# A decoder block with a routed expert layer: router moved into the cross-attention stage, token rows gathered in place of scattered

## The chip, the cores and the metric

The kernel runs on one core of a Trainium2 chip. The metric is the device time of one execution in microseconds (us), as the median of repeated runs. Within 0.2% a run of this kernel can't be told from no change.

## The reference

32 sequences of 112 tokens, 512 channels, all f32:

```python
x = x + attn(layernorm(x))                    # windowed attention, 16 heads of 32
x = x + xattn(layernorm(x), ctx_1024)         # 16 query heads of 128, 8 key heads, 375 context rows of 256
h = layernorm(x).reshape(-1, 512)             # 3584 tokens
probs = softmax(h @ wg)                       # wg: 512 x 8
idx = argmax(probs);  gate = probs[idx]
x = x + gate * (h @ W[idx].T + b[idx])        # W: 8 x 512 x 512, one expert per token
```

## The kernel before

The program is three functions, one after the other, each a block of its own: on every engine its instructions are written out in order, and between functions all engines meet at a barrier and the semaphores are cleared.

`window_attention` does the first line in 8 turns of 4 sequences and stores the sum `x1` and its normalized transpose `h2T` in DRAM. Beside that it clears things for the last stage: `clear_slots` stores 1032 KB of blank rows into `slots` once in each turn.

`cross_attention` (L847) goes twice over the 32 sequences, 8 query heads in each half, so 64 batches of 4 steps, 256 steps. A product is made of three passes over high and low halves of its operands. A step has on TensorE, in this order: the scores of 2 heads (`scores`), the K projection of the next batch (`early_fills`), a part of the output projection of a finished 128-token tile (`rows`, with the parts placed by `ROWS_AT`), the product with V of step i - 2 (`pv`), further fills (`late_fills`, `before_transposes`), the transposes of the probabilities of step i - 1 (`probsT`), and at times one more fill behind them (`behind_transposes`). Fills are the transposes of the context (C, only in the first half), and the projections K, V and Q. They go in turns through two PSUM banks, in the fixed list `ORDER`: a fill waits on TensorE until the one two places before it has been copied out by ScalarE (high half) and VectorE (low half). The two context transposes of a batch are one in step g = 2 and one in step g = 3. `HEAD` is what is made before step 0. `splits_at` spreads the splitting of weights into halves; the output weights are split in batch 0. The softmax goes from VectorE (`maxima`) to GpSimd (bias), ScalarE (`exps`), VectorE (`inverses`), GpSimd (L1201, two multiplications) and back to TensorE. When a tile's output projection is whole, `add` (L1307) adds it to `sums`; in the first half the sum is kept in `x1_half`, in the second half it goes to `x2`. All its loads and stores are issued by SyncE, in a loop over batches: `load_base`, `load_x`, `load_ctxT`, `store`, `load_mask`, and others, each behind its wait.

`expert_ffn` (L1533) has two blocks. The first reads `x2` back (28 tiles of 128 tokens, loops over pairs), normalizes it (L1736 to L1757), transposes it (L1862) and multiplies it with `wg` (L1872, f32, 8 columns); it finds the expert, the gate and the slot of each token in a chain of small VectorE operations (L1809 to L1846) in which each waits for the one before; scatters the 28 tiles of token rows with GpSimd to `slots` in DRAM, sorted by expert (L1683); and beside that loads, transposes and splits the expert weights `W` in 32 units of 256 KB through 4 buffers (L1624, L1888, L1702, L1779). The second block loads the 35 slots of 128 rows with SyncE (L1966), normalizes (L2008), transposes (L2052), splits (L1996, L2013), multiplies with the expert's weights (L2063), adds bias (L2023), gate and residual (L2028), and scatters the result to `out` (L1980).

```python
                        sp.dma_start(rows[:, k, :], slots_t[bass.ds(n, 1)].rearrange("a p c -> (a p) c")) \
                            .then_inc(rows_in[k], 16)
                        if is_first(turn, k, U) and k == 3:
                            sp.dma_start(bias[:] ...
```

## Time and profile before

| | us |
|---|---|
| median of 3 runs (2679.69 to 2681.14) | 2681.05 |
| the profiled execution, its own time | 2699.72 |
| its span, first to last instruction | 2698.0 |
| TensorE matmul busy | 2495.8 (93%) |
| TensorE weight loads busy | 2270.3 (84%) |
| VectorE busy | 1743.5 (65%) |
| ScalarE busy | 1248.4 (46%) |
| GpSimd busy | 1014.3 (38%) |
| mean DMA rate | 81 GB/s |

PE is TensorE's matmuls, PEld its weight loads, DVE VectorE, ACT ScalarE, POOL GpSimd, SP SyncE, and SPq SyncE's queue of DMA issues. PEclk is the granted TensorE clock, 1.00 being 2.4 GHz and 0.50 being 1.2 GHz. In a timeline row the numbers are the start and the length in us, then engine, line, operation, what it writes<-what it reads, the count, and in brackets the engine's idle time just before and what ended it.

### The profile page before, as it was taken

Reading aid. Unit: us, or ns where it says so; the run is one execution under the profiler, and the core shown is the slowest. Engines: PE = TensorE matmul, PEld = TensorE weight load, DVE = VectorE, ACT = ScalarE, POOL = GpSimd, SP = SyncE. Lnnn points to the kernel's source line nnn. Section 1 sums busy time; section 2 is a strip of 40 time slices with the busy share of each in tenths; the row PEclk is TensorE's granted clock in tenths of the full one; section 3 lists DMA queues with packets and bytes.
Section 4 is the critical chain, followed back from the end, with each engine's and each line's share of the span. In section 5 each row is a group of like instructions: output and inputs, shape, how many; then the busy total and the mean of one; then the engine's idle time right before and its main releaser. Section 6 shows DMA issues by size and latency. Waiting matters only on the chain. (4 is left out here: it accounts for less than half of the span.)

```text
span 2698.0 us, 46191 instructions
## 1 busy us (share of the span) xinstructions
PE 2495.8 (93%) x14850; PEld 2270.3 (84%) x14851; DVE 1743.5 (65%) x4871; ACT 1248.4 (46%) x3155; POOL 1014.3 (38%) x1424
## 2 busy tenths in 40 slices
PE   6999997699999999999999999999999999979388
PEld 5888886589998998999888889989999998969276
DVE  6878886475666657565666657566575656654466
ACT  4545554354544545454554545454454545522211
POOL 3434443043333434343333434344343434431422
PEclk9999999899999999999999999999999999985699
DMA  7322232422121221121132212111121111122654
GB/s 255 95 70 84 93 103 93 142 62 66 56 62 48 87 66 59 55 73 66 49 107 61 82 50 61 50 53 58 41 66 54 41 58 50 44 70 75 217 178 129
DMA packets 110493, 217.89 MB, mean 81 GB/s; under 512 B 20400, under 2 KB 50832, under 8 KB 110016
## 3 DMA queue, kind: packets, MB, share of 16 engines
q1 hardware_dynamic: 105040, 188.42, 22.3%
q0 software_dynamic: 5040, 16.58, 1.6%
q10 hardware_dynamic: 224, 10.49, 1.2%
q8 instruction: 105, 1.72, 0.3%
q14 instruction: 84, 0.69, 0.1%
HBM read 134.57 MB, written 91.36 MB: 84 GB/s over the span
## 5 line engine op out<-in xcount | busy, mean ns | idle before, releaser
L1201 POOL TENSOR_SCALAR x_probs<-x_probs,x_inv 112x376 f32<-112x376 f32 x512 | 634.6, 1249 | 196.0 <-DVE x_inv L1352 196.0
L1245 ACT ACTIVATE x_probs<-x_probs,x_bias 112x376 f32<-112x376 f32 x512 | 307.9, 602 | 426.8 <-POOL x_bias L1195 426.8
L1195 POOL TENSOR_SCALAR x_bias<-x_top 112x1 f32<-112x1 f32 x512 | 118.0, 230 | 973.8 <-DVE x_top L1324 973.8
L1410 PE MATMUL x_ps_f<-x_xT,x_wq 128*128 128x448 f32 x1536 | 342.4, 373 | 7.1 <-DVE x_wq L1292 6.4
L1456 PE MATMUL x_ps_r<-x_wo,x_oT 128*128 128x512 f32 x1344 | 345.6, 393 | 2.3 <-DVE x_wo L1292 1.4
L1410 PE MATMUL x_ps_f<-x_wv,x_ctxT 128*128 128x512 f32 (+1 forms) x1152 | 308.5, 405 | 25.4 <-DVE x_kT L1302 22.8
L1410 PEld LDWEIGHTS x_ps_o<-x_pT,x_v 128*128 128x128 f32 (+1 forms) x2304 | 295.3, 191 | 35.2 <-DVE x_pT L1331 17.4
L1410 PE MATMUL x_ps_s<-x_kT,x_qT 128*112 128x376 f32 x1536 | 313.8, 340 | 3.0 <-DVE x_top L1324 3.0
L1410 PEld LDWEIGHTS x_ps_f<-x_xT,x_wq 128*128 128x128 f32 x1536 | 282.6, 190 | 36.1 <-DVE x_v L1302 6.9
L1410 PE MATMUL x_ps_f<-x_ctxT,x_wk 128*128 128x376 f32 x1536 | 308.7, 337 | 4.2 <-DVE x_kT L1302 3.0
L1410 PE MATMUL x_ps_o<-x_pT,x_v 128*128 128x224 f32 (+1 forms) x2304 | 300.3, 275 | 11.6 <-DVE x_pT L1331 11.6
L1456 PEld LDWEIGHTS x_ps_r<-x_wo,x_oT 128*128 128x128 f32 x1344 | 251.2, 189 | 40.7 <-DVE x_wo L1292 1.7
L1410 PEld LDWEIGHTS x_ps_f<-x_ctxT,x_wk 128*128 128x128 f32 x1536 | 271.1, 190 | 6.5 <-DVE x_kT L1302 4.8
L1410 PEld LDWEIGHTS x_ps_s<-x_kT,x_qT 128*112 128x112 f32 x1536 | 259.2, 176 | 17.5 <-issue 4.0
L1324 DVE CUSTOM_DVE_ANT_0 x_probs<-x_ps_s,x_mrow 112x376 f32<-112x376 f32 x512 | 259.0, 543 | 5.7 <-DVE x_mrow L1312 5.7
L1410 PEld LDWEIGHTS x_ps_f<-x_wv,x_ctxT 128*128 128x128 f32 (+1 forms) x1152 | 202.3, 188 | 69.3 <-DVE x_kT L1302 28.8
L1331 DVE TENSOR_TENSOR x_pT<-x_ps_t,x_pT 128x336 fp32r<-128x336 f32 x512 | 234.1, 499 | 0.1
L1302 DVE TENSOR_TENSOR x_qT<-x_ps_f,x_qT 128x448 fp32r<-128x448 f32 x128 | 80.0, 625 | 234.0 <-ACT x_qT L1221 234.0
L1349 DVE TENSOR_SCALAR x_total<-x_total 112x1 f32<-112x1 f32 x512 | 78.9, 154 | 221.6 <-ACT x_probs L1245 221.6
L1302 DVE TENSOR_TENSOR x_v<-x_ps_f,x_v 128x512 fp32r<-128x512 f32 (+1 forms) x192 | 132.8, 691 | 121.2 <-ACT x_v L1221 121.0
L1228 ACT ACTIVATE x_pT<-x_ps_t 128x336 fp32r<-128x336 f32 x512 | 202.6, 453 | 0.0
L1221 ACT ACTIVATE x_v<-x_ps_f 128x512 fp32r<-128x512 f32 (+1 forms) x192 | 115.0, 599 | 161.9 <-PE x_ps_f L1410 161.7
(186 smaller groups left out, 3833.6 us busy)
## 6 DMA issues: line engine op xcount, KB each, us to landing
x_ctxs<-x_ctxT SPq DMA_DIRECT2D x32, 752.0 KB, 4.1
x_ctxT<-x_ctxs SPq DMA_DIRECT2D x32, 752.0 KB, 4.7
x_xT<-h2T SPq DMA_DIRECT2D x16, 896.0 KB, 4.9
m_rows<-slots SPq DMA_DIRECT2D x35, 258.0 KB
slots<-w_blank SPq DMA_DIRECT2D x8, 1032.0 KB, 5.2
x_ctxn<-in_ctx_dram SPq DMA_DIRECT2D x32, 256.0 KB
m_hn<-in_L_ffn_W_dram SPq DMA_DIRECT2D x32, 256.0 KB
w_xa<-in_x_dram SPq DMA_DIRECT2D x32, 224.0 KB, 3.5
```

The source lines that it names most:

```text
L1195: pool.tensor_scalar(bias[:, m:m + 1], top[:, m:m + 1], -0.1 * NEG, -SCALE, ALU.max, ALU.mult) \
L1201: pool.tensor_scalar(probs[0:T, m, 0:SE], probs[0:T, m, 0:SE], inv[:, m:m + 1], None, ALU.mult).then_inc(normed, 1)
L1221: act.activation(dst[HI], src, ACT.Copy).then_inc(fill_hi, 1)
L1228: act.activation(pT[:, HI, :, h * T:(h + 1) * T], ps_t[h][:, 0:NKC * T].rearrange("p (c t) -> p c t", c=NKC), ACT.Copy).then_inc(pT_hi, 1)
L1245: act.activation(probs[0:T, m, 0:SE], probs[0:T, m, 0:SE], ACT.Exp, bias=bias[:, m:m + 1], scale=SCALE, accum_out=total[:, m:m + 1]).then_ ...
L1302: dve.tensor_tensor(dst[LO], src, dst[HI].bitcast(F32), ALU.subtract).then_inc(fill_done, 1)
L1324: dve.tensor_tensor_reduce(out=probs[0:T, m, 0:SE], in0=ps_s[h][0:T, 0:SE], in1=mrow[:, i // G % 2, :], scale=1.0, scalar=-3.0e38, op0=ALU ...
L1331: dve.tensor_tensor(pT[:, LO, :, h * T:(h + 1) * T], ps_t[h][:, 0:NKC * T].rearrange("p (c t) -> p c t", c=NKC), pT[:, HI, :, h * T:(h + 1 ...
L1349: dve.tensor_scalar(total[:, m:m + 1], total[:, m:m + 1], 1e-30, None, ALU.max) \
L1410: last = pe.matmul(out, w, r, start=m == 0, stop=m == len(jobs) - 1)
L1456: last = pe.matmul(ps_r[:], oT[:, a, h, slot:slot + P], wo[:, b_, h, :], start=h == 0 and (a, b_) == PASSES[0], stop=h == H - 1 and (a, b_ ...
```

## The change

- In the second half of `cross_attention` each finished tile is, in the step after `add`'s and later ones, also measured (`stats`), normalized (`rstd` on GpSimd, `normal`), transposed (fill R, one step later), multiplied with `wg` (fill L, three steps later), and its gate made (`keep_logits`, `gate_weights`, `gate`, four steps later). Row, mean, 1/deviation and gate are stored together in `x2r` (515 columns), two batches later in SyncE's loop; `load_base` comes at the end of the loop's body. R and L are fills in `ORDER` and take turns in the two PSUM banks. The last tiles are finished in a `TAIL` of seven more steps, and the logits stay in SBUF.
- Both context transposes of a batch are in step g = 2. `HEAD` makes all eight Q fills ahead of the context transposes of batch 1, and the first of them starts by chunks, each chunk of `xT` and `wq` split together. The output weights are split in batch 1.
- `expert_ffn` is one block without loops. It starts with the chain of small operations, inverts the permutation with 28 TensorE products of one-hot bf16 matrices, and gathers each slot's rows from `x2r` with GpSimd, 8 slots ahead, by the same index by which it scatters the result. `W` is loaded from the start of the block; the bias is loaded behind `W`.
- `window_attention` no longer clears `slots`; it stores four blank blocks of `x2r` and `out` near its end.

The core of the diff:

```diff
-                        if s == 2:
-                            clear_slots(turn)
...
+                for n in range(rest.shape[0] // P):
+                    sp.dma_start(blanks[n * P:(n + 1) * P, :], blank[:]).then_inc(blank_out, 16)
+                    sp.dma_start(rest[n * P:(n + 1) * P, :], blank[:, 0:C]).then_inc(blank_out, 16)
...
+    def tiles_at(i):
+
+        if i == STEPS + 2:
+            return [TILES - 1]
+        return [tile - TILES for tile, h0, h1 in (row_parts(i) if 0 <= i < STEPS else []) if h1 == H and tile >= TILES]
...
-        if g >= 2 and b + 2 < B:
-            out.append(("C", b + 2, g - 2))
+        if g == 2 and b + 2 < B:
+            out += [("C", b + 2, 0), ("C", b + 2, 1)]
         if g == 3 and b + 1 < NB:
             out.append(("V", b + 1, 0))
         if g == 1:
             out += [("V", b, c) for c in range(1, NKC)]
+        out += [("R", t, 0) for t in tiles_at(i - 1)] + [("L", t, 0) for t in tiles_at(i - 3)]
...
-        return fs if fs and fs[-1][0] == "C" else fs[:-1]
+        return fs if fs and fs[-1][0] in "CRL" else fs[:-1]
...
-    HEAD = [("C", 0, 0), ("C", 0, 1)] + [("K", 0, g) for g in range(G)] + [("Q", 0, h) for h in range(4)] + \
-           [("C", 1, 0), ("C", 1, 1)] + [("Q", 0, h) for h in range(4, H)] + [("V", 0, 0)]
-    ORDER = HEAD + [f for i in range(STEPS) for f in early_fills(i) + late_fills(i)]
+    HEAD = [("C", 0, 0), ("C", 0, 1)] + [("K", 0, g) for g in range(G)] + [("Q", 0, h) for h in range(H)] + \
+           [("C", 1, 0), ("C", 1, 1), ("V", 0, 0)]
+    TAIL = range(STEPS, STEPS + 7)
+    ORDER = HEAD + [f for i in range(STEPS) for f in early_fills(i) + late_fills(i)] + \
+            [f for i in TAIL for f in after(i)]
...
-        if b == 0:
+        if b == 1:
...
+                        t = tile - TILES
+                        sp.wait_ge(gate_ready, t + 1)
+                        sp.dma_start(result[t * P:(t + 1) * P, :], sums[:, tile % 2, :]).then_inc(stored[tile % 2], 16)
...
+                    if b - 2 in TILE_OF and TILE_OF[b - 2] >= TILES:
+                        store(TILE_OF[b - 2])
...
+                    if b in TILE_OF and TILE_OF[b] >= TILES:
+                        load_base(TILE_OF[b])
...
+                    pool.tensor_scalar(var, var, EPS, None, ALU.add).then_inc(ve_ready, 1)
+                    pool.wait_ge(ve_ready, t + 1)
+                    pool.tensor_tensor(var, var, power[:], ALU.pow).then_inc(rs_ready, 1)
...
+                    act.activation(weight_of[:], logits[:, t, :], ACT.Exp, bias=less[:, 1:2], scale=1.0,
+                                   accum_out=sums[:, t % 2, GATE:GATE + 1]).then_inc(weights_ready, 1)
...
+                        act.activation(hT, ps_f[bank_of(f)][:].rearrange("p (c t) -> p c t", c=KC), ACT.Copy) \
+                            .then_inc(hT_ready, 1)
...
+                def stats(t):
+                    row = sums[:, t % 2, :]
+                    dve.wait_ge(rows_added, TILES + t + 1)
+                    dve.bn_stats(st[:], row[:, 0:C]).then_inc(st_ready, 1)
+                    dve.wait_ge(st_ready, t + 1)
+                    dve.bn_aggr(row[:, MEAN:RSTD + 1], st[:]).then_inc(mv_ready, 1)
+
+                def normal(t):
+                    row = sums[:, t % 2, :]
+                    dve.wait_ge(rs_ready, t + 1)
+                    if t:
+                        dve.wait_ge(fill_ready, until(("L", t - 1, 0)))
+                    dve.tensor_scalar(hn, row[:, 0:C], row[:, MEAN:MEAN + 1], row[:, RSTD:RSTD + 1],
+                                      ALU.subtract, ALU.mult).then_inc(hn_ready, 1)
+
+                def keep_logits(t):
+                    dve.wait_ge(fill_ready, until(("L", t, 0)))
+                    if t:
+                        dve.wait_ge(weights_ready, t)
+                    dve.tensor_copy(logits[:, t, :], ps_f[bank_of(("L", t, 0))][:, 0:E]).then_inc(logit_kept, 1)
+                    dve.wait_ge(logit_kept, t + 1)
+                    dve.tensor_reduce(less[:, 0:1], logits[:, t, :], AX.X, ALU.max).then_inc(top_ready, 1)
+                    dve.wait_ge(top_ready, t + 1)
+                    dve.tensor_scalar(less[:, 1:2], less[:, 0:1], -1.0, None, ALU.mult).then_inc(less_ready, 1)
+
+                def gate(t):
+                    g = sums[:, t % 2, GATE:GATE + 1]
+                    dve.wait_ge(weights_ready, t + 1)
+                    dve.reciprocal(g, g).then_inc(gate_ready, 1)
...
+                    for t in tiles_at(i - 1):
+                        normal(t)
                     inverses(i)
...
+                        held = ORDER[PLACE[f] - BANKS]
+                        if held[0] == "R":
+                            pe.wait_ge(hT_ready, held[1] + 1)
+                        elif held[0] == "L":
+                            pe.wait_ge(logit_kept, held[1] + 1)
+                        else:
+                            pe.wait_ge(fill_done, halved(held))
...
+                    elif kind == "R":
+                        pe.wait_ge(hn_ready, at + 1)
+                        for c in range(KC):
+                            last = pe.transpose(out[:, c * P:(c + 1) * P], hn[:, c * P:(c + 1) * P], ident[:])
+                    elif kind == "L":
+                        pe.wait_ge(wg_in, 16)
+                        pe.wait_ge(hT_ready, at + 1)
+                        last = product(out[:, 0:E], [(hT[:, c, :], wgs[:, c, :]) for c in range(KC)])
...
+                        for c in range(KC):
+                            if n == 0:
+                                weights("q", at * QUAD // B, c)
+                                pe.wait_ge(x_lo, KC * at + c + 1)
...
+                for i in TAIL:
+                    for f in after(i):
+                        fill(f)
+                    if i == STEPS:
+                        pv(STEPS - 1)
+                        rows(HALVES * TILES - 1, 0, H)
...
+                for u in range(UNITS):
+                    e, o = divmod(u, KC)
+                    if u >= 4:
+                        sp.wait_ge(w_ready, u - 3)
+                    sp.dma_start(wn[:, u % 4, :], W[e, o * P:(o + 1) * P, :]).then_inc(w_in[u % 4], 16)
+                sp.dma_start(bias[:].rearrange("p e o -> p (e o)"),
+                             b.rearrange("e o -> (e o)").rearrange("(a n) -> a n", a=1)
+                             .to_broadcast([P, E * C])).then_inc(bias_in, 16)
...
+                def gather(k):
+                    pool.indirect_dma_start(out=rows[:, k % U, :], out_offset=None, in_=x2r,
+                                            in_offset=bass.IndirectOffsetOnAxis(ap=index[:, k:k + 1], axis=0)) \
+                        .then_inc(rows_in[k % U], 16)
...
+                for k in range(SLOTS):
+                    pool.wait_ge(y_ready, k + 1)
+                    pool.indirect_dma_start(out=out, out_offset=bass.IndirectOffsetOnAxis(ap=index[:, k:k + 1], axis=0),
+                                            in_=y[:, k % Y, :], in_offset=None).then_inc(out_done[k % Y], 16)
+                    if k + U < SLOTS:
+                        gather(k + U)
...
+                in_tile, of_tile = slotf[:, 0], slotf[:, 1]
+                link(dve.tensor_scalar(of_tile, best[:], 1.0 / P, 0.5 / P - 0.5, ALU.mult, ALU.add))
+                link(dve.tensor_scalar(of_tile, of_tile, 12582912.0, None, ALU.add))
+                link(dve.tensor_scalar(of_tile, of_tile, -12582912.0, None, ALU.add))
+                link(dve.scalar_tensor_tensor(out=in_tile, in0=of_tile, scalar=-float(P), in1=best[:],
+                                              op0=ALU.mult, op1=ALU.add))
+                dve.wait_ge(iota_done, 6)
...
+                link(dve.tensor_tensor(at_tile[:, :, 1, :], kinds[:].unsqueeze(1).to_broadcast([P, TILES, SLOTS]),
+                                       of_tile.unsqueeze(2).to_broadcast([P, TILES, SLOTS]), ALU.is_equal))
+                dve.tensor_tensor(at_tile[:, :, 0, :], at_tile[:, :, 1, :],
+                                  tile1[:].unsqueeze(2).to_broadcast([P, TILES, SLOTS]), ALU.mult)
+                link(dve.tensor_scalar(at_tile[:, :, 1, :], at_tile[:, :, 1, :], own[:, 0:1], None, ALU.mult))
+                for t in range(TILES):
+                    dve.tensor_scalar(at_lane[:, t, :], lane[:], in_tile[:, t:t + 1], None, ALU.is_equal) \
+                        .then_inc(lanes_ready, 1)
...
+                dve.wait_ge(inverted, 1)
+                a, b_ = ps_i[:, 0:SLOTS], ps_i[:, SLOTS:2 * SLOTS]
+                dve.scalar_tensor_tensor(out=found[:, 0, :], in0=a, scalar=0.0, in1=spare[:, 0:SLOTS],
+                                         op0=ALU.is_equal, op1=ALU.mult)
+                dve.tensor_scalar(found[:, 1, :], a, float(P), -float(P), ALU.mult, ALU.add)
...
+                dve.tensor_copy(index[:], found[:, 0, :]).then_inc(index_ready, 1)
+                for u in range(UNITS):
+                    low_w(u)
...
+                for u in range(4):
+                    transpose_w(u)
...
+                for t in range(TILES):
+                    pe.wait_ge(lanes_ready, t + 1)
+                    last = pe.matmul(ps_i[:, 0:2 * SLOTS], at_lane[:, t, :], at_tile[:, t].rearrange("p a k -> p (a k)"),
+                                     start=t == 0, stop=t == TILES - 1)
+                last.then_inc(inverted, 1)
+                for u in range(4, UNITS):
+                    transpose_w(u)
...
+                    pe.wait_ge(h_ready, k + 1)
+                    pe.wait_ge(w_lo, UNITS)
...
```

## Rows read from the trace of the kernel before

**Rows 1.** Busy time by stretch: PE, PEld, DVE, ACT, POOL, PEclk, DMA share, GB/s.
```profile
1370.00:2404.00 1034.00, 1014.04 (x6048) 927.81 (x6048) 652.75 (x2038) 511.26 (x1402) 419.93 (x570) 0.99 0.18 54
...
2430.00:2494.00 64.00, 62.77 (x301) 62.67 (x300) 31.50 (x96) 13.81 (x26) 10.97 (x20) 0.50 0.23 73
2508.00:2550.00 42.00, 12.46 (x53) 9.23 (x54) 9.72 (x15) 7.44 (x13) 25.97 (x27) 0.54 0.75 245
2580.00:2690.00 110.00, 108.61 (x534) 88.48 (x532) 83.63 (x134) 19.16 (x32) 32.71 (x34) 1.00 0.47 145
```

**Rows 2.** Timeline, marks of the expert stage: its start, first chain step, places, first split.
```profile
2413.05 0.20 POOL L41 MEMSET m_ident<- 128x128 f32 x1 [20.62 <-POOLq L58]
...
2495.37 0.39 DVE L1809 TENSOR_REDUCE m_best<-m_logits 128x28 f32<-128x224 f32 x1 [0.59 <-POOL m_hT L1677]
...
2505.29 0.18 DVE L1841 CAST m_slot<-m_slotf 128x28 uint32<-128x28 f32 x1
...
2507.13 2.48 DVE L1779 TENSOR_TENSOR m_wT<-m_a,m_wT 128x512 f32 x4 [0.39 <-DVE m_owner L1846]
```

**Rows 3.** Groups by line and shape: busy us, mean ns of one, idle before.
```profile
L1843 DVE TENSOR_TENSOR m_hT<-m_hT,m_number 128x280 f32<-128x280 f32 x1 | 0.4, 442 | 0.0
L1802 DVE COPY m_order<-m_before 128x128 f32<-128x128 f32 x1 | 0.2, 227 | 0.0
```

**Rows 4.** Expert weights and scatter: timeline, and one line's ns min/median/max.
```profile
2549.51 0.60 ACT L1702 ACTIVATE m_wT<-m_a 128x512 f32 x1 [1.68 <-PE m_a L1888]
...
2564.98 0.60 ACT L1702 ACTIVATE m_wT<-m_a 128x512 f32 x1 [0.54 <-PE m_a L1888]
...
L1683 POOL DMA_INDIRECT slots<-m_tokens,m_slot x28: 959/963/1227, 2506.5 to 2540.9; - x28
```

**Rows 5.** The slots: timeline of bias and first products, and the scatter's line.
```profile
2568.53 0.43 SPq L1969 DMA_DIRECT2D m_bias<-in_L_ffn_b_dram  x1
...
2577.80 0.55 DVE L2008 TENSOR_SCALAR m_h<-m_rows 128x512 f32<-128x512 f32 x1 [5.25 <-DMA m_bias<-in_L_ffn_b_dram]
...
2579.18 3.06 PE L2063 MATMUL m_y<-m_wT,m_rT 128*128 x12
...
L1980 POOL DMA_INDIRECT out_dram<-m_y,m_rows x35: 962/962/964, 2581.2 to 2691.1; - x35
```

**Rows 6.** Timeline of the head and first batch of the cross stage.
```profile
492.80 12.48 PE L1410 MATMUL x_ps_f<-x_xT,x_wq 128*128 128x448 f32 x48 [6.40 <-DVE x_wq L1292]
...
528.46 1.06 ACT L1210 ACTIVATE x_wo<-x_wo 128x1024 fp32r<-128x1024 f32 x1 [2.62 <-DMA x_wo<-own_wo]
...
533.89 2.91 PE L1410 MATMUL x_ps_f<-x_wv,x_ctxT 128*120 128x512 f32 x6 [5.19 <-DVE x_kT L1302]
```

**Rows 7.** Waits of PE, 640 to 1370, then 1370 to 2400: us, times, longest.
```profile
PE x_ps_f L1410 <- DVE x_kT L1302: 10.5, 21, 1.4
...
PE x_ps_o L1410 <- DVE x_pT L1331: 9.6, 10, 1.7
```

**Rows 8.** Timeline: router products at 1.2 GHz, then three transposes at 2.4 GHz.
```profile
2435.99 3.54 PEld L1872 LDWEIGHTS m_l<-m_wgs,m_hT 128*128 128x128 f32 x16
...
590.54 0.49 PE L1422 MATMUL x_ps_f<-x_ident,x_ctxn 128*128 128x128 f32 x3
590.87 0.74 PE L1482 MATMUL x_ps_t<-x_ident,x_probs 112*128 112x112 f32 x6
```

**Rows 9.** Timeline of one step's softmax on POOL and when TensorE takes it.
```profile
2363.87 2.48 POOL L1201 TENSOR_SCALAR x_probs<-x_probs,x_inv 112x376 f32<-112x376 f32 x2 [0.76 <-DVE x_inv L1352]
...
2369.18 0.61 PEld L1482 LDWEIGHTS x_ps_t<-x_ident,x_probs 112*128 112x128 f32 x6
```

**Rows 10.** Timeline: last output projection, and first pair of tiles from measuring to logits.
```profile
2400.71 8.36 PE L1456 MATMUL x_ps_r<-x_wo,x_oT 128*128 128x512 f32 x24 [0.87 <-DVE x_oT L1340]
...
2417.51 1.29 DVE L1736 BATCH_NORM_STATS2 m_st<-m_tokens 128x6 f32<-128x512 f32 x2 [4.33 <-DMA m_tokens<-x]
...
2429.64 0.17 DVE L1763 COPY m_logits<-m_l 128x16 f32<-128x16 f32 x1 [2.55 <-PE m_l L1872]
```

More of the change, by code:

```diff
@@ L857, in _, with cross_attention @@
                         fill(Turn(TURNS), f)
[L860 removed]
+def cross_attention(nc, B, T, S, h2T, ctx, mask, Wq, Wk, Wv, Wo, wg, base, mid, result, room):
     D = 128
@@ L1391, in _ @@
                         split(p)
+                    for t in tiles_at(i - 4):
+                        gate(t)
                 out(STEPS - 2)
                 probsT(STEPS - 1)
-                out(STEPS - 1)
-                add(HALVES * TILES - 1)
+                for i in TAIL:
+                    for f in after(i):
+                        fill(f)
+                    for t in tiles_at(i - 1):
+                        normal(t)
+                    for t in tiles_at(i - 4):
+                        gate(t)
+                    if i == STEPS:
+                        out(STEPS - 1)
+                    for t in tiles_at(i):
+                        add(TILES + t)
+                        stats(t)
             @block.tensor
@@ new lines, in expert_ffn @@
+        wn = sb("wn", [P, 4, C])
+        bias = sb("bias", [P, E, C])
+        rows = sb("rows", [P, U, R])
+        h = sb("h", [P, 2, C])
+        rT = sb("rT", [P, 2, 2, KC, P], F32R)
+        y = sb("y", [P, Y, C])
+        ident = sb("ident", [P, P])
+        owner = sb("owner", [P, SLOTS], I32)
+        index = sb("index", [P, SLOTS], U32)
+        order = sb("order", [P, TILES, E])
+        before = sb("before", [P, TILES, E])
+        like = sb("like", [P, TILES, E])
+        places = sb("places", [P, TILES, E])
@@ new lines, in expert_ffn @@
+        best = sb("best", [P, TILES])
+        chosen = sb("chosen", [P, TILES, E], BF16)
+        slotf = sb("slotf", [P, 2, TILES])
+        number = sb("number", [P, 2, 1, E])
+        start = sb("start", [P, E])
+        ownerf = sb("ownerf", [P, SLOTS])
+        steps = sb("steps", [P, SLOTS, E])
+        ends = sb("ends", [P, SLOTS, E])
+        lower = sb("lower", [P, P], BF16)
+        ones = sb("ones", [P, P], BF16)
+        lane = sb("lane", [P, P])
+        kinds = sb("kinds", [P, SLOTS])
```

813 lines of the change are left out of this document (305 added, 508 removed).

## The prediction

> **What bounds the kernel now.** I read the busy time by stretch first, then the waits inside each stretch, then timelines. The second half of the cross stage is TensorE's: matmuls are busy 1014 of 1034 us at a granted clock of 0.99, VectorE and ScalarE are at 63% and 49%, and the transfers at 54 GB/s. What is added to TensorE there costs its own time. The expert stage is another matter [rows 1]: from 2430 to 2494 TensorE is full but at 0.50, the 1.2 GHz level, with the router; from 2508 to 2550 every engine is mostly idle while DMA is busy at 0.75 (scatter and weights); from 2580 to 2690 TensorE is full again at 2.4 GHz with the slots. The marks of the stage [rows 2]: it starts at 2413.05, the chain of small operations at 2495.37, the places are written at 2505.29, and the span ends at 2698.0. So the stage lasts 285 us and 82 of them pass before its chain begins.
>
> The sum is made against the profiled execution, 2699.7 us by its own time and 2698.0 in span. The median of the runs is 2681.05, so I scale the result by 2681.05 / 2699.72 = 0.9931.
>
> **Expert stage, removed and added.** The new stage starts at once with the chain. (a) Chain to the places: 9.9 us [rows 2]; two operations go (the sum of the exponentials and its reciprocal), but they stand beside the ranking products, so I take nothing off. (b) Added behind it, all on VectorE, all waited for: four operations on 28 columns, taken at 0.2 each, 0.8; three of 128x980 at 0.442 us for 280 columns and about 1.04 ns for each further one, 1.17 each, 3.5 in sum [rows 3]; 28 comparisons of 128x128, taken like the copy of that size, 0.23 us, less what overlaps, 0.2 each, 5.6 [rows 3]; the owner's four operations, which before ended at 2507.1, 1.8; six last ones for the index, 1.1. The 28 bf16 products run beside the comparisons. So the index is ready 22.7 us after the start. Bounds: the 28 comparisons overlap fully at 0.1 us, or take 0.3 each: 20 to 26. (c) Weights: the first four units wait, transposed, for VectorE's low halves: 2.5 us. The other 28 go at the pace of the copies from 2549.51 to 2564.98, 15 units in 15.5 us or 1.03 each, 28.9 us [rows 4]. (d) The first 8 gathers are issued now. 28 scatters of the same size cost the weights a lot: from 2508 to 2550 some 8 units passed in 42 us [rows 1, 4], so (42 - 8) / 28 = 1.2 us for each DMA, which makes 9.7 for 8. At the other end it is nothing, since at the pace above the transfers had room. I take the middle, 5. Sum to the last unit: 22.7 + 2.5 + 28.9 + 5 = 59.1. (e) From the last copy of a unit (2565.6) to the second slot's product (2579.18) there were 13.6 us, of which 5.25 were VectorE's wait for the 2 MB of bias, 9.2 us after their issue [rows 5]. The bias is now issued some 4 units before the end and lands while the first product runs, so 8.3 remain. (f) From there to the end, 118.8 us, nothing changes: the slots follow each other at (2691.1 - 2581.2) / 34 = 3.23 us [rows 5], TensorE's own time at 0.99 of the stretch [rows 1]. GpSimd now issues a gather beside each scatter: 2 x (0.96 + 0.3 that I assume between two) = 2.5 us, still under 3.23.
>
> VectorE works 83.6 of the 110 us of the slots, and all 35 scatter issues lasted 962 to 964 ns [rows 1, 5]: nothing held them. Against this change speaks the Trainium skill, "SBUF — State Buffer", section "Who interferes with whom": a VectorE copy or tensor_scalar in its two-port mode locks GpSimd out, which then can't write the descriptors of its DMAs, so row loads moved from SyncE to GpSimd lose their immunity. No row shows a scatter lengthened so; what it would make is the third rival.
>
> Stage: 59.1 + 8.3 + 118.8 = 186.2 in place of 285.0: **minus 98.8**. Ends: -84 (comparisons 0.3, contention 9.7, the bias again in the way) and -107.
>
> **First half of the cross stage.** TensorE stood 6.4 us for the last piece of the first query weights and 5.2 us in batch 0, since ScalarE waited for `wo`'s transfer (2.6 us) and VectorE stood behind it [rows 6]. The first Q fill now follows the chunks (VectorE needs 1.8 us for a chunk of `xT` and `wq`), which starts it some 3 us earlier but leaves it in pieces; I take 4 for the whole head, with the value weights' split now early. The `wo` splits in batch 1 no longer wait for a transfer: 5. The V fill in step g = 3 waited for the K fill two places before it, 21 times, 10.5 us in all from 640 to 1370 [rows 7]; with C, C in g = 2 that V has free banks, and the second C comes behind the three-head part of the output projection (some 2 us of TensorE), except in batches without a tile: 8 of the 10.5. Together **minus 17**, ends 0 (the waits return one step earlier) and -25. The blank stores gone from the window stage free no engine that anyone waits for: 0; they run beside a TensorE that is busy 0.9 of that stage.
>
> **Second half of the cross stage.** Each tile adds to TensorE 4 transposes and 4 f32 products of 8 columns, which are 8 weight passes. At 1.2 GHz 16 passes took 3.54 us, 0.221 each, and at that level the weight load, not the 8 columns, is the time; at 2.4 GHz I take half, 0.11. Three transposes at 2.4 GHz took 590.87 - 590.54 = 0.33 us, also 0.11 each [rows 8]. So 12 x 0.11 = 1.32 us for a tile, and for the 26 tiles not in the tail 34.3. Low end: 9.6 us of waits for `pT` [rows 7] lie in this half and could take up 8 of it: +26. High end: the passes cost at 2.4 GHz what they cost at 1.2, 12 x 0.221 = 2.65: +69. I take **plus 35**. What hides the rest: VectorE gets 2.2 us and ScalarE 1.2 a tile in 37 us. `normal` (0.54 us, between `maxima` and `inverses`) lies where VectorE waits for ScalarE's exponentials. GpSimd's `rstd` (about 1 us) stands behind the two multiplications, and the next bias behind it, so the next softmax is 0.3 us late; the row that ends at 2366.35 is taken by TensorE at 2369.18 [rows 9], so there are 2.8 us of cover. R and L fill a bank each; a K fill behind L now waits for the K fill before it, covered by the output projection. On SyncE the store two batches later waits for a gate made in the step in which the mask load behind it waits anyway, and the base load is 2.5 steps early.
>
> **Tail.** R of tile 26 stands before the last `pv`, and the last tile has to pass through measuring, GpSimd, R, ScalarE, L, exponential, reciprocal and store before the barrier. Before, the pair of tiles took 2429.64 - 2417.51 = 12.1 us from measuring to logits [rows 10], with another pair's work between; for one tile I take 8, plus 1.2 for gate, plus L of tile 26 and its logits ahead of the last `add` 1.6, plus 2.4 for R before `pv`: **plus 13**. Base load 55 now waits for the store of tile 53, which is late, but the last projection takes 8.4 us at the low clock [rows 10] and covers it; if it doesn't, +3. Ends 9 and 17.
>
> **Sum.** -98.8 - 17 + 35 + 13 = -67.8: 2699.7 - 67.8 = 2631.9 profiled, times 0.9931 = 2613.7. I say **2613** (-2.5%).
>
> **Rivals.** First, the added weight passes or their bank waits cost double (2.65 us a tile): +34, 2647. For it: the router was only seen at 1.2 GHz. Against it: transposes do halve. Second, gathers and weights collide as the scatter did, and instruction loading with them: the weights go at a third of their pace while the gathers are under way, +15, 2628. For it: 2508 to 2550. Third, GpSimd becomes the bound of the slots: a gather takes 2 us to issue rather than 0.96, or is held up by VectorE, and the period is 3.6 in place of 3.23, from about 2.0 us per gather on; 27 slots x 0.35 = +10, 2623. Fourth, other side: TensorE stands at R for `hn`. VectorE holds `inverses` back behind `normal`, which waits for `rstd`, which waits for the multiplications; once that is longer than the 2.8 us of cover [rows 9] every tile pays. It is slower than before when a tile pays over 67.8 / 28 = 2.4 us beyond the cover; at 4 us it gives 2681 + 44 = 2725. Against it: the mean arrives in the step of `add`, and VectorE waits there anyway. Fifth, the regrouped context fills and the head bring nothing, because the wait for K moves with the C fill: 2630.
>
> **How the numbers follow.** Main case 0.58, first rival 0.12, second 0.10, third 0.05, fourth 0.04, fifth 0.11. All but the fourth are faster by over 1%. Ends of the terms: best -107 - 25 + 26 + 9 = -97, 2585; worst without a rival about -84 - 5 + 45 + 17 = -27, 2654. Not all go one way: 2590 to 2648 holds the main case, the second, third and fifth rivals and just the first. About 0.2% (5 us) is what can be told from no change. Faster 0.95, same 0.01, slower 0.04.
>
> **What would show it.** Expert stage 186 us, with the index about 23 us after its start, the last weight unit at 59, slots at 3.23, gather issues at 0.96. R and L together 1.3 us a tile at clock 1.00, and no wait of TensorE for `hn` or `hT`. Second half 35 us longer. No 5 us wait in batch 0, and few K waits from batch 2 on. The tail some 13 us longer from the last projection to the barrier. A second half longer by 60 us, a slot period over 3.3, or a weight phase of 50 us would prove steps of the sum wrong.

## The result: 48 us faster, 19 less than forecast

| | us |
|---|---|
| kernel before, median of 4 runs beside the changed one | 2680.37 (2677.56 to 2681.14) |
| changed kernel, median of 4 runs | 2632.25 (2630.38 to 2634.80) |
| ratio | 0.9817, 95% interval 0.9803 to 0.9830 |
| forecast | 2613, range 2590 to 2648 |
| changed kernel, profiled execution and its span | 2631.62 and 2629.9 |

The profile of the changed kernel, busy time by stretch (PE, PEld, DVE, ACT, POOL, PEclk, DMA share, GB/s). The stretches are the second half of the cross stage, the weights behind the index, and the slots; they answer to the first, third and fourth row of [rows 1].
```profile
1356.00:2388.00 1032.00, 1015.38 (x6186) 932.50 (x6186) 681.43 (x2160) 522.65 (x1441) 433.24 (x606) 1.00 0.17 54
2466.00:2500.00 34.00, 23.17 (x112) 16.41 (x110) 20.25 (x31) 16.73 (x28) 6.99 (x8) 0.72 0.85 286
2511.00:2621.00 110.00, 107.31 (x528) 87.46 (x526) 82.48 (x131) 19.23 (x32) 61.41 (x62) 1.00 0.46 147
```
The router's stretch at 0.50 is gone; what lies between the index and the slots is 34 us with the transfers at 0.85. GpSimd in the slots went from 33 to 61 us of 110, and TensorE stayed the bound.

Timeline marks of the expert stage, which answer to [rows 2, 5]: its first operation, the index, the last low half of a weight unit, the second slot's product.
```profile
2443.84 0.39 DVE L1834 TENSOR_REDUCE m_best<-room 128x28 f32<-128x224 f32 x1 [3.93 <-PEq L58]
...
2464.64 0.18 DVE L1893 CAST m_index<-m_found 128x35 uint32<-128x35 f32 x1
...
2499.43 0.69 DVE L1831 TENSOR_TENSOR m_wT<-m_y,m_wT 128x512 fp32r<-128x512 f32 x1 [1.06 <-ACT m_wT L1796]
...
2508.78 3.05 PE L1975 MATMUL m_y<-m_wT,m_rT 128*128 x12
```
From 2443.8, the last unit is done at 56.3 us and the second product starts at 64.9; the stage ends after 186.1.

Timeline of TensorE in one tile's part of the second half, at 2.4 GHz: the router's product (L) and what follows it, the transposes (R) and what follows them; [rows 8] had only neighbours of both.
```profile
2102.21 0.96 PE L1524 MATMUL x_ps_f<-room 128*128 128x8 f32 x8
2103.03 0.77 PE L1613 MATMUL x_ps_t<-x_ident,x_probs 112*128 112x112 f32 x6
...
2115.84 0.60 PE L1547 MATMUL x_ps_f<-x_ident,room 128*128 128x128 f32 x4
2116.28 0.74 PE L1613 MATMUL x_ps_t<-x_ident,x_probs 112*128 112x112 f32 x6
```
L takes 2103.03 - 2102.21 = 0.82 us and R 0.44, 1.26 a tile, and neither waits.

Timeline of the head and batch 0 (beside [rows 6]), and the waits of TensorE from 640 to 1360 (beside the first row of [rows 7]; us, times, longest):
```profile
492.61 18.94 PE L1573 MATMUL x_ps_f<-x_xT,x_wq 128*128 128x448 f32 x87 [0.18 <-DVE x_wq L1357]
...
524.10 1.66 PE L1524 MATMUL x_ps_f<-x_wv,x_ctxT 128*120 128x512 f32 x6 [1.77 <-DVE x_kT L1402]
```
```profile
PE x_ps_f L1542 <- DVE x_kT L1402: 6.1, 3, 2.0
PE x_ps_f L1573 <- DVE x_ctxT L1402: 5.0, 6, 0.8
PE x_ps_o L1524 <- DVE x_pT L1431: 0.7, 3, 0.3
```
The 5.2 us wait of batch 0 is 1.8 and its V fill comes 9.8 us earlier. The 21 waits of V for K are gone, but three waits of the context fill for K and six of a query fill for the context have come, 11.1 us in all where there were 10.5.

Timeline of the tail, beside [rows 10]: the last `pv`, the last output projection, the last R and the last gate.
```profile
2412.90 2.02 PE L1524 MATMUL x_ps_o<-x_pT,x_v 128*128 128x224 f32 x9 [2.65 <-DVE x_pT L1431]
...
2422.64 7.72 PE L1587 MATMUL x_ps_r<-x_wo,x_oT 128*128 128x512 f32 x24 [0.87 <-DVE x_oT L1440]
...
2434.98 1.08 PE L1547 MATMUL x_ps_f<-x_ident,room 128*128 128x128 f32 x4 [3.84 <-DVE room L1376]
...
2439.74 0.16 DVE L1392 RECIPROCAL x_sums<-x_sums 128x1 f32<-128x1 f32 x1 [0.46 <-ACT x_weight_of L1265]
```

**The two profiles set against each other.** I followed the 512 reciprocals of the softmax, one by one, through both traces. At the start of batch 2 the changed kernel leads by 10.9 us, at the start of the second half by 16.3 (1475.42 against 1491.73), at the last reciprocal it is 17.7 behind (2407.93 against 2390.28), and at the start of the expert stage 30.8 behind (2443.84 against 2413.05). The stage then takes 186.1 in place of 285.0. The spans differ by 68.1; the sum of the prediction was 67.8. Yet the medians differ by 48.1. So the sum was right against the execution that it was read from, and what needs explaining is that execution: it lasted 18.7 us longer than the median of its kernel, while that of the changed kernel lies at its median.

### The profile page after: what moved, and what is told of

It reads as the page before. It is cut to its first block and busy times, and to the rows that moved or that the text cites. A ratio compares the mean times of both kernels' runs of the same rounds, so it can differ in the third digit from the quotient of the medians.

```text
span 2629.9 us, 45420 instructions
## 1 busy us (share of the span) xinstructions
PE 2462.5 (94%) x14878; PEld 2236.7 (85%) x14878; DVE 1762.0 (67%) x4977; ACT 1259.5 (48%) x3210; POOL 1033.3 (39%) x1462
## 5 line engine op out<-in xcount | busy, mean ns | idle before, releaser
L1237 POOL TENSOR_SCALAR x_bias<-x_top 112x1 f32<-112x1 f32 x512 | 123.4, 241 | 955.6 <-DVE x_top L1424 955.3
L1573 PE MATMUL x_ps_f<-x_xT,x_wq 128*128 128x448 f32 x1536 | 343.5, 373 | 12.7 <-DVE x_ctxT L1402 5.8
L1524 PEld LDWEIGHTS x_ps_o<-x_pT,x_v 128*128 128x128 f32 (+1 forms) x2304 | 296.4, 192 | 30.4 <-DVE x_pT L1431 12.7
L1279 ACT ACTIVATE x_qT<-x_ps_f 128x448 fp32r<-128x448 f32 x128 | 69.8, 545 | 256.2 <-PE x_ps_f L1573 256.2
L1613 PE MATMUL x_ps_t<-x_ident,x_probs 112*128 112x112 f32 x1536 | 190.5, 260 | 0.0
```

What stands on the lines that cost most here:

```text
L1237: pool.tensor_scalar(bias[:, m:m + 1], top[:, m:m + 1], -0.1 * NEG, -SCALE, ALU.max, ALU.mult) \
L1524: last = pe.matmul(out, w, r, start=m == 0, stop=m == len(jobs) - 1)
L1573: last = pe.matmul(out[:, 0:T4], wq[:, a, c, n * D:(n + 1) * D], xT[:, b_, c, :], start=c == 0 and (a, b_) == PASSES[0], stop=c == KC - 1 ...
L1613: last = pe.transpose(ps_t[h][:, c * T:(c + 1) * T], probs[0:T, n % 4, c * P:(c + 1) * P], ident[0:T, 0:T])
```

## The experiments

Times are medians. Four variants shared each of three chips with runs of the kernel before: 2682.1 on the first chip (2681.0 without one of the 15 runs, which took 7992.6), 2697.3 on the second, 2679.2 on the third. Variants of the changed kernel are set against the 2632.3 us of the result, on the third chip against its 2634.0 there. Of these variants only the one of the context fills edits the part ahead of the second half; yet the profiles of the others stand 0.5 to 4.7 us behind that of the changed kernel at that point, and its own second profile 1.9. So effects of a few us are read inside the traces.

### Where the surplus of the first profile lies

**The kernel before, profiled again** (first chip), no edit.

> The kernel before, unchanged, profiled again. Its profiled execution of the prediction lasted 2699.7 us, 18.7 above the median of its runs, while that of the changed kernel (2631.6) lies at its median; against the profiled one the sum of the prediction (-67.8) meets the difference of the spans (-68.1). Theory A: the 18.7 us lie in the router's part of the expert stage, which in the first profile ran at 1.2 GHz from its start to its end (82 us before the chain); in a typical run it gets 2.4 GHz for a part of it, so that the new profile, at about 2681, has the chain some 64 us after the stage's start and everything else within 1 us. Theory B: they are spread over the cross stage and the slots (the factor 0.993 that I used); then every stretch is 0.7% shorter and the router's part is still 81 to 82 us.

The median is 2680.2, the profiled execution took 2685.4 with a span of 2683.6. Both theories fell. Every mark of the cross stage stands 1.2 to 1.3 us earlier from batch 2 to its end, a constant, so nothing is spread; and the chain starts 81.6 us after the stage's start, with the clock at 0.50 all the way. The difference is in the timeline of the weights, chain start and last low half:
```profile
2493.39 0.39 DVE L1809 TENSOR_REDUCE m_best<-m_logits 128x28 f32<-128x224 f32 x1 [0.58 <-POOL m_hT L1677]
...
2550.98 0.69 DVE L1779 TENSOR_TENSOR m_wT<-m_a,m_wT 128x512 f32 x1 [0.55 <-ACT m_wT L1702]
```
and in the busy time of 2508 to 2550, to be read beside the third row of [rows 1]:
```profile
2508.00:2550.00 42.00, 25.71 (x104) 18.79 (x102) 18.14 (x27) 15.52 (x26) 24.22 (x26) 0.52 0.94 315
```
The last unit came 58.3 us after the chain's start, against 71.1 in the first profile: 12.8 of the 14.4 us between the two spans. The same scatters were under way, but the transfers moved 315 GB/s against 245, and ScalarE made 26 copies in that stretch against 13. The waits of the same phase, the first profile's (2507 to 2566), then the second's (2505 to 2551):
```profile
PE m_a L1888 <- DMA m_hn<-in_L_ffn_W_dram: 33.6, 19, 8.7
...
ACT m_wT L1702 <- DMA x_wo<-own_wo: 16.6, 3, 9.9
```
```profile
PE m_a L1888 <- DMA m_hn<-in_L_ffn_W_dram: 15.6, 12, 3.5
```
TensorE waited 33.6 us for weights against 15.6. ScalarE's 16.6 us, put down to a transfer long done, are missing in the second; what it stood for there the trace does not say. On the second chip all nine runs of the kernel before took 2693.1 to 2698.3, so a time near that of the first profile is the rule on one chip; whether the first profile was taken on such a chip, nothing here tells. The other three runs on record with it took 2679.7 to 2681.1. The second profile too lies 5.2 us above its median, and no trace tells where.

**The kernel before without its scatters** (second and third chip).

```diff
-                    for t in range(TILES):
+                    for t in range(1):
                         pool.indirect_dma_start(out=slots, ...
-                    pool.wait_ge(scattered, 16 * TILES)
+                    pool.wait_ge(scattered, 16)
```

> The kernel before with 27 of its 28 scatters to the slots left out (the slots keep their blank rows, so the expert stage works on blanks; all its matmuls, copies and transfers are there). Both theories on the router's clock fell with the second profile of the kernel before: its router lasted 81.6 us again, all at 1.2 GHz, and the 14.4 us by which that execution was shorter lie between the chain and the last weight unit (58.3 us after the chain's start in place of 71.1), where scatters and weights run side by side. Theory A: this collision is what varies, and in a median run of before it costs some 12 us over weights alone (28 units at 1.03 us from the chain's end on, last unit some 43 to 46 us after the chain's start): the kernel without scatters takes 2664 to 2669 us. Theory B: the weights are slow there for another reason (the clock at 1.2 GHz, first instructions of the block), and nothing changes: 2680.

> The kernel before with 27 of 28 scatters left out, once more, for the case that this chip is one on which before takes 2680. Theory A as above: 2667 again whatever before takes, 13 us under a 2680 or 30 under a 2697. Theory B: it moves with before, 2650 beside a 2680.

27 of the 28 scatters are left out, so the experts work on blank rows. 2667.3 beside a before of 2697.3 (ratio 0.9890, 0.9875 to 0.9905), and 2669.4 beside 2679.2 (0.9954, 0.9939 to 0.9970). Theory A holds both times for the kernel without scatters; it had their price at some 12 us, and on the second chip it is 30. From the second chip, first and last low half, and the busy time:
```profile
2506.50 2.48 DVE L1779 TENSOR_TENSOR m_wT<-m_a,m_wT 128x512 f32 x4 [0.39 <-DVE m_owner L1846]
...
2538.89 0.69 DVE L1779 TENSOR_TENSOR m_wT<-m_a,m_wT 128x512 f32 x1 [0.65 <-ACT m_wT L1702]
```
```profile
2508.00:2550.00 42.00, 27.01 (x130) 19.43 (x128) 21.89 (x33) 17.93 (x30) 0.00 (x0) 0.80 0.71 232
```
The last unit is 44.8 us after the chain's start (2494.73). In both profiles of the kernel before, the stretch from the last unit to the end is as long as here (131.6 and 132.0 us, here 131.2), so what the scatters cost lies ahead of the last unit. So the collision of scatters and weights costs 30 us on one chip and 10 on another, and nearly all that these chips differ by in the kernel before (18 us, without scatters 2 the other way) goes with the scatters. Why it costs more on one chip, no run shows.

**The changed kernel again** (third chip), no edit.

> The changed kernel, unchanged, beside the kernel before on the same chip. The kernel before took 2680 us on the chip of the result and of its second profile, but 2697 on the chip of the last four runs, which is the time of its first profile (2700). Theory A: what differs between chips is the collision of scatters and weights alone, which the changed kernel does not have; it takes 2632 on any chip, so that the gain is 65 us beside a 2697 and 48 beside a 2680. Theory B: the chips differ in other stretches too, and the changed kernel moves with them (2648 beside 2697).

2634.0 beside 2679.2 (0.9820, 0.9806 to 0.9833); in its profile the stage takes 187.5 us, and the cross stage is 1.7 to 1.9 us later from its first softmax on. The changed kernel itself was not run on the second chip, but its variant with late gathers was, at 2633.6. That one has no gathers beside the weights; the variant with late rstd, also on the second chip, has them, and there the last unit comes 55.9 us after the stage's start, as on the first chip (56.3). So the changed kernel's time doesn't follow the chip as before's does.

### The steps of the sum

**Gathers held back** (second chip).

```diff
                 pool.wait_ge(index_ready, 1)
+                pool.wait_ge(w_lo, UNITS - 6)
                 for k in range(U):
```

> The changed kernel with its first 8 gathers held back until 26 of the 32 weight units are split. It prices the contention that the prediction put at 5 us (0 to 9.7). Theory A (the gathers cost the weights about 0.6 us each): the last weight unit comes at 51 to 52 us after the stage's start in place of 56.3, the first slot waits a little for its row, and the whole is 2 to 4 us faster, 2629. Theory B (the weights are held by their own four buffers and by SyncE): last unit still at 55 to 56, the whole 0 to 3 us slower.

2633.6. The timeline, index and last low half:
```profile
2465.82 0.18 DVE L1894 CAST m_index<-m_found 128x35 uint32<-128x35 f32 x1
...
2495.61 0.69 DVE L1832 TENSOR_TENSOR m_wT<-m_y,m_wT 128x512 fp32r<-128x512 f32 x1 [0.62 <-ACT m_wT L1797]
```
The last unit comes at 51.3 in place of 56.3 (start at 2445.0), so 8 gathers cost the weights 5.0 us, as the prediction had it (in the other profiles that keep this part as it is, the last unit comes at 55.7 to 58.3, so 4.4 to 7.0); but TensorE then waits 8.5 us for the first row, and the second product starts at 66.1, not 64.9. The size of theory A and the end of theory B.

**Context fills apart again** (first chip).

```diff
-        if g == 2 and b + 2 < B:
-            out += [("C", b + 2, 0), ("C", b + 2, 1)]
+        if g >= 2 and b + 2 < B:
+            out.append(("C", b + 2, g - 2))
```

> The changed kernel with its two context fills in the steps g = 2 and g = 3 again, as before the change. The prediction had 8 us for the regrouping. The softmaxes of the two profiles drift apart by only 2 us from batch 2 to batch 14, since waits for K in front of V (10.5 us) are gone but 11 us of waits for K in front of C and for ctxT in front of Q have come. Theory A (waits only moved): 0 to 4 us slower than the changed kernel, 2632 to 2636. Theory B (the regrouping is worth 8, and something else in the first half eats 6): 2640.

2636.8, 4.5 above the 2632.3 of the changed kernel, just above theory A's span. Its profile says more: the old wait is back to the number,
```profile
PE x_ps_f L1524 <- DVE x_kT L1402: 10.5, 21, 1.4
```
and its softmaxes fall behind those of the changed kernel from 1.7 us at the first to 8.1 in batch 34, then stay there (my expectation miscounted: its 2 us are from batch 2 to batch 28). That is 6.4, of which 3.3 come in batches 26 to 32. Two variants that leave this half alone also fell behind in it, by 2.9 us, so the regrouping is worth some 4 to 6. The span is only 4.1 us longer, since the expert stage, which the edit doesn't touch, was 2.0 shorter in this profile.

**Transposes twice, router's product twice** (first chip).

```diff
-                        for c in range(KC):
+                        for c in [c for _ in range(2) for c in range(KC)]:
                             last = pe.transpose(...
```
```diff
+                        product(out[:, 0:E], [(hT[:, c, :], wgs[:, c, :]) for c in range(KC)])
                         last = product(out[:, 0:E], [(hT[:, c, :], wgs[:, c, :]) for c in range(KC)])
```

> The changed kernel with the four transposes of each tile's normalized rows done twice. It prices the transposes in the second half. Theory A (TensorE's own time, 0.11 us a pass at 2.4 GHz): 28 x 0.44 = 12 us slower than the changed kernel, 2644. Theory B (bank waits and late softmaxes hide or double part of it): under 5 or over 20 us.

> The changed kernel with the router's product of each tile done twice (the second writes the same values). Its text has four products of 128x8, but the profile counts eight passes, 0.82 us in all. Theory A (the weight load of each pass is the time, 0.10 us, whatever the 8 columns): 28 x 0.82 = 23 us slower, 2655. Theory B (the eight columns cost little and the passes overlap their neighbours): under 12 us.

2645.0 and 2658.4, that is +12.7 and +26.1 over 2632.3, against 12 and 23. Inside the traces, over 21 tiles (batches 36 to 60), R twice costs 0.38 us a tile and L twice 0.81; 16 passes of the product in a row take 1.71:
```profile
2117.12 1.86 PE L1524 MATMUL x_ps_f<-room 128*128 128x8 f32 x16
2118.83 0.77 PE L1614 MATMUL x_ps_t<-x_ident,x_probs 112*128 112x112 f32 x6
```
Against 0.44 and 0.82 for a single set, the passes cost TensorE nearly all or all of their own time, eight columns or not. The rest of the +26.1 is 3 us that this execution was late before batch 32 already, in a part without L.

**rstd made late** (second chip).

```diff
                     pool.wait_ge(mv_ready, t + 1)
+                    for _ in range(5):
+                        idles[0] += 1
+                        pool.tensor_tensor(st[:, 6:7], power[:], power[:], ALU.pow).then_inc(idled, 1)
+                        pool.wait_ge(idled, idles[0])
                     pool.tensor_scalar(var, ...
```

> The changed kernel with five more operations of one column (powers, about 0.6 us each, 3 us in all) ahead of each tile's rstd on GpSimd. It tries the rival on the other side: normal waits for rstd on VectorE, inverses behind it, and TensorE takes the multiplied row 2.8 us after it is made. Theory A (2.8 us of cover, as in the prediction): about as slow as before by 28 x (3.0 + 0.3 - 2.8) = 14 us at most, 2632 to 2646. Theory B (the bias behind rstd has no cover, every tile pays all 3 us): 28 x 3 = 84 us, 2716.

2640.1, +7.9, theory A. In the trace the five powers (0.556 us each) cost the 24 tiles of the second half up to batch 60 only 3.0 us together, and what comes after that 3.7, most of it in the tail, where the longest wait of TensorE for a normalized tile went from 3.8 to 7.0 us:
```profile
PE x_ps_f L1554 <- DVE room L1383: 8.4, 3, 7.0
```
Another 4.6 us by which this profile is late stand ahead of the second half, where no rstd is made. The rival on the other side had cover to spare: 3 us more for each tile cost 0.13 a tile where tiles follow each other, and all 3 for the last tile, where none follows.

**GpSimd kept busy in the slots** (third chip).

```diff
                         .then_inc(rows_in[k % U], 16)
+                    idles[0] += 1
+                    pool.memset(idle[:], 1.0).then_inc(idled, 1)
+                    pool.wait_ge(idled, idles[0])
```

> The changed kernel with a fill of 128x1024 on GpSimd behind each gather (I put it at 1 to 1.5 us; the profile will tell), which tries the rival in which GpSimd becomes the bound of the slots. With it GpSimd has about 1.05 + 0.97 + 2 x 0.3 + 1.3 = 3.9 us for each of the 27 slots that gather, over TensorE's 3.23. Theory A (the bound moves to GpSimd once the eight rows and four results ahead are used up): the end comes 27 x (3.9 - 3.23) = 18 us later less the few us by which TensorE was ahead, so 10 to 18 us slower than the changed kernel, and the last waits of the slots are for GpSimd. Theory B (the buffers ahead cover it to the end): under 5 us.

2639.7, +5.7 over the 2634.0 on the same chip: between the two. GpSimd's timeline tells why:
```profile
2560.40 1.00 POOL L1792 DMA_INDIRECT out_dram<-m_y,m_index  x1 [0.28 <-POOL m_idle L1784]
2561.70 0.97 POOL L1780 DMA_INDIRECT m_rows<-x2r,m_index  x1 [0.30 <-issue]
2562.67 0.97 POOL L1784 MEMSET m_idle<- 128x1024 f32 x1
2563.92 1.00 POOL L1792 DMA_INDIRECT out_dram<-m_y,m_index  x1 [0.28 <-POOL m_idle L1784]
```
The fill took 0.97, not 1.3, and starts with no gap, so a slot costs GpSimd 2563.92 - 2560.40 = 3.52 us. TensorE's period is 3.5 as well from the third slot to about the 30th, then 3.24 again, and 27 x (3.52 - 3.24) = 7.6 of the 7.7 us by which the slots are longer (from the second slot's product to the end). Theory A's mechanism with a price that I had set too high: the bound moves at once, the rows and results ahead cover nothing, and the changed kernel stands 0.6 us a slot away from it (1.04 + 0.97 + 2 x 0.30 = 2.6 against 3.24).

### A better order

**Low halves among the chain**: 20 units between the chain's steps (second chip), then 7 more among the comparisons (third chip).

```diff
                     ins.then_inc(chain, 1)
+                    if count[0] >= 9 and lows[0] < EARLY:
+                        low_w(lows[0])
+                        lows[0] += 1
                     dve.wait_ge(chain, count[0])
...
-                for u in range(4):
+                for u in range(EARLY + 4):
                     transpose_w(u)
```
```diff
                         .then_inc(lanes_ready, 1)
+                    if t % 4 == 3:
+                        low_w(lows[0])
+                        lows[0] += 1
```

> The changed kernel with VectorE's low halves of the first 20 weight units placed between the steps of the chain of places, so that the weights are loaded while the chain runs, and only 12 units come behind the index. Theory A (VectorE's order is what holds the weights back): the index is ready 20.8 + 20 x 0.69 = 34.6 us after the stage's start, the last unit 12 x 1.03 later at 47 us in place of 56.3, so 9 us faster than the changed kernel, 2623. Theory B (the weights are held by their transfers, which stop and go at some 1.2 us a unit, and the gathers now come later): last unit at 53 or later, under 4 us faster.

> The kernel with the low halves of 20 weight units among the steps of the chain, and 7 more among the 28 comparisons, one after each fourth, so that 5 are left behind the index. Theory A (VectorE's sum of work sets the end of the weights): the index at 34.9 + 7 x 0.69 = 39.7 us after the stage's start, the last unit 5 x 1.03 later at 44.9 in place of 47.1, 2 us faster than with 20, 2623. Theory B (the rows' gathers, issued 5 us later, or the bias behind the weights now set the first slots): the last unit is earlier but the second slot's product is not, no gain.

2625.0 (forecast 2623) and 2621.0 (forecast 2623), the latter 0.9779 of before (0.9766 to 0.9792) and 13.0 under the changed kernel on the same chip. With 20 units ahead the index is ready at 35.1 us and the last unit at 47.1, as worked out (34.6 and 47). With 27 the index comes at 40.0:
```profile
2484.51 0.18 DVE L1904 CAST m_index<-m_found 128x35 uint32<-128x35 f32 x1
2484.60 0.68 DVE L1838 TENSOR_TENSOR m_wT<-m_y,m_wT 128x512 fp32r<-128x512 f32 x1
2485.20 1.28 DVE L1838 TENSOR_TENSOR m_wT<-m_t,m_wT 128x512 fp32r<-128x512 f32 x2
2486.40 1.31 DVE L1838 TENSOR_TENSOR m_wT<-m_y,m_wT 128x512 fp32r<-128x512 f32 x2
2488.76 0.55 DVE L1912 TENSOR_SCALAR m_h<-m_rows 128x512 f32<-128x512 f32 x1 [1.05 <-DMA m_rows<-x2r,m_index]
```
The last five units follow at VectorE's own pace, 43.1 us after the stage's start at 2444.66, and now it waits for a gathered row: what was hidden behind the weights is the next wait. This is the fastest version of the study.

## Why the prediction was right where it was, and where it was not

**Held.** The sum of -67.8 against the profiled execution (measured -68.1), and its four terms:

| term | forecast | measured |
|---|---|---|
| expert stage | 186.2 | 186.1 |
| first half of the cross stage | -17 | -16.3 |
| second half | +35 | +34.0 |
| tail | +13 | +13.1 |

That the two sums differ by 0.3 us is in part luck, since inside the terms errors of 1 to 3 us cancel. In the stage: index 21.0 after 22.7 forecast (the last of the three wide operations, bf16 to bf16, took 0.49, not 1.17, and the owner 1.4, not 1.8), weights 35.3 behind it for 36.4, 8.7 to the second product for 8.3, and 121.1 from there for 118.8. Of those 2.3 us, 2.8 lie after the last scatter's issue (2620.2 to the end at 2629.9, against 2691.1 to 2698.0). They are in an instruction of GpSimd's sequencer that closes its block, the `DRAIN`. The view of that line, for the changed kernel, the second and the first block of the kernel before, and that first block without scatters (ns):
```profile
L1741 POOLq DRAIN  x1: 5774/5774/5774, 2623.3 to 2623.3; - x1
L1956 POOLq DRAIN  x1: 2913/2913/2913, 2694.1 to 2694.1; - x1
L1603 POOLq DRAIN  x1: 2352/2352/2352, 2544.4 to 2544.4; - x1
L1603 POOLq DRAIN  x1: 148/148/148, 2509.3 to 2509.3; - x1
```
These blocks issue 70, 35, 28 and 1 indirect transfers, so the closing takes some 0.08 us for each, and the barrier behind it waits for that. The 35 gathers, in place of loads issued by SyncE, cost 2.9 us there; the prediction had "nothing changes". The slots' period is 3.24.

In the first half the terms cancel too: head and batches 0 and 1 gave 10.9 for 9, and from batch 2 to the second half 5.4 came for 8. But the reason given for those 8 fell. The 10.5 us of waits for K did go, and about as much (11.1) came back ahead of the context and query fills, as in the fifth rival; 3.4 of the 5.4 came in the last three batches of that half, and which wait they are no view shows.

In the second half the passes took 0.105 us (1.26 / 12) for 0.11, and no wait of TensorE for a normalized tile lasted over 0.8 us outside the tail. The first and fourth rivals did not come about, nor did the second beyond the 5 us that the sum had. Neither did the third: the gathers' issues took 0.97 us. The scatters' took 1.04 in the median beside 0.96 before,
```profile
L1785 POOL DMA_INDIRECT out_dram<-m_y,m_index x35: 969/1039/1058, 2510.2 to 2620.2; - x35
```
with VectorE as busy as before. That is all that the trace shows of a hold on GpSimd. By the rule of the Trainium skill that the prediction weighed ("SBUF — State Buffer", section "Who interferes with whom") the issues could have been locked out while VectorE copies in its two-port mode; here the issues are 0.08 us longer in the median, and TensorE's period of 3.24 does not feel it. Which of VectorE's operations in the slots use that mode the trace does not tell, so no run here tries the rule itself.

**Failed: the step from the sum to the median.** I wrote that I "scale the result by 2681.05 / 2699.72 = 0.9931", as if the surplus of the profiled execution were spread over everything. It was not. Of the 14.4 us between the two profiles 12.8 sat where scatter and weights ran side by side, most of it in the 42 us of [rows 1], a part that the change takes out; the other 4.3 of the 18.7 no trace here places. So the "minus 98.8" counted time that an execution at the median doesn't spend, and nothing was to be scaled: 2699.7 - 67.8 = 2631.9, or 2681.05 - 67.8 + 18.7, is the measured time. The factor 0.9931 took off 18 of the 19 us that are missing. The signs were there: the stretch that I myself called a collision had waits of 9 to 10 us on three engines, and nothing else in the trace was irregular. The "1.2 us for each DMA" was a misreading: [rows 1] has 13 copies of ScalarE in the 42 us, not "some 8 units", and (42 - 13) / 28 is 1.04. Without scatters the weights gain 26.3 us on the first profile and 13.5 on the second, 0.94 and 0.48 for each of 28, and the gathers cost 5.0 / 8 = 0.6. So the 5 us of the sum, a middle between 0 and 9.7, was a lucky choice.

**Where the gain comes from.** The second profile of the kernel before is the fairer base; it lies 5 us above its median. From it to the changed kernel the cross stage is 32.0 us longer (stage start at 2411.8, then 2443.8) and the expert stage goes from 271.8 to 186.1. Of those 85.7 us, 81.6 are the router with what stood ahead of the chain; 2.0 lie between the chain's start and the last weight, where 13.5 of collision are gained, 5.0 go to the gathers and, by difference, 6.5 to the longer way to the index; 4.4 lie between the last weight and the second product, mostly the wait for the bias (5.6 in that profile, 0.4 now); and 2.3 are lost at the end, where GpSimd's closing takes 2.9 more. So the change buys 82 us of router (with the reading back of `x2` ahead of it, at 1.2 GHz from 2420 on) for 34 us of router at 2.4 GHz and 13 of tail, and the first half gives 15 beside that. On a chip where the collision costs 30 it gains some 64.

## What to carry to other kernels

Before scaling a sum from one profiled execution to the median, ask where that execution's surplus lies: if it sits in a phase that the change removes, it is subtracted from the gain, not shared out. Here it was a phase in which many small indirect transfers ran beside a bulk load, and its cost differed threefold between chips. And when a chain of small operations on one engine stands ahead of a bulk job of the same engine, put the bulk job's pieces between the links: that gave 13 us here for a few lines. Moving loads to an engine's indirect transfers also lengthens that engine's closing, which counts where it ends the kernel.

## What the runs showed of the hardware

- The same kernel took 2679 to 2682 us on two chips and 2697 on a third, a difference that vanished with its 27 scatters of 128 rows (2667 and 2669). The changed kernel took 2632 and 2634 on two chips, its variant with late gathers 2634 on the third.
- f32 products of eight columns cost 0.10 us a pass at 2.4 GHz, about as much as a 128x128 transpose at 0.11. What both have is the load of 128x128 weights; that it is the price is inferred from this.
- A bf16 to bf16 tensor_scalar of 128x980 took 0.49 us where comparisons and products of that size took 1.18.
- A GpSimd fill of 0.97 us behind a DMA issue starts without the 0.30 us gap that stands between two issues.
- GpSimd's closing `DRAIN` of a block took 0.15, 2.35, 2.91 and 5.77 us behind 1, 28, 35 and 70 indirect transfers.
